# The transposes of the attention probabilities move behind the projections of queries and keys within a slot

## What is computed

```python
def attention(q, k, v, mask):
    scores = jnp.einsum('bhqd,bhkd->bhqk', q, k) / jnp.sqrt(jnp.float32(HD))
    scores = scores * mask - 10000.0 * (1.0 - mask)
    probs = jax.nn.softmax(scores, axis=-1)
    return jnp.einsum('bhqk,bhkd->bhqd', probs, v)
ln_out = layernorm(hidden_states, ln1_s, ln1_b)
q, k, v = jnp.split(ln_out @ w_qkv + b_qkv, 3, axis=-1)
x = hidden_states + merge_heads(attention(..q, k, v.., ltor_mask)) @ w_ao + b_ao
ln_out = layernorm(x, ln2_s, ln2_b)
q = ln_out @ w_q + b_q
k, v = jnp.split(encoder_states @ w_kv + b_kv, 2, axis=-1)
x = x + merge_heads(attention(..q, k, v.., cross_mask)) @ w_co + b_co
ln_out = layernorm(x, ln3_s, ln3_b)
return x + gelu(ln_out @ w1 + b1) @ w2 + b2
```

## The kernel before

| engine | order |
|---|---|
| TensorE | scores, **transposes**, flips of slots 5 and 6, weighing, flip of the context (2, 3), queries (0, 2, 4) or keys (1, 3, 7), flip of slot 4, outputs, values, keys of slot 5, queries of slot 6 |
| ScalarE | top of the values, output row, **high half of the probabilities**, high halves of flips, bias and exponentials, high half of queries or keys, middle of the values, flip of slot 4, high halves of keys of slot 5 and queries of slot 6 |
| VectorE | maxima, mask, norm (4), **low half of the probabilities**, statistics (1, 2), low halves of flips, context, low half of queries or keys, flip of slot 4, low halves of keys of slot 5 and queries of slot 6, centre (1, 3), norm (3) |

## Time and profile before

### The profile page before, as it was taken

One profiled execution on the slowest core, in us unless ns is written; L12 is line 12 of the kernel. 1 busy time (PEld: TensorE's weight loads), 2 busy tenths in 40 slices (PEclk: granted clock), 3 DMA queues, 4 the chain that ended last, 5 costly groups with the idle time before them and its releaser, 6 DMA issues. The chain is left out here.

```text
span 2081.6 us, 39412 instructions
## 1 busy us (share of the span) xinstructions
PE 1957.9 (94%) x12304; PEld 1657.1 (80%) x12304; DVE 1390.2 (67%) x2571; ACT 1072.6 (52%) x2562; POOL 884.1 (42%) x910
## 2 busy tenths in 40 slices
PE   5999999999998999999999999699999999999999
PEld 5788888888787778887887887588888888888887
DVE  6889889888888998899889888662322323232221
ACT  4666666667667666666676666443222222222222
POOL 5556556556557655555565555450201012020110
PEclk9999999999999999999999999899999999999999
DMA  6332222222223432332232224501010101101010
GB/s 172 94 91 70 65 77 68 66 72 74 61 73 88 106 97 73 86 93 72 77 96 71 73 83 104 165 28 51 11 55 5 60 12 48 50 10 54 6 41 21
DMA packets 144820, 141.51 MB, mean 68 GB/s; under 512 B 20736, under 2 KB 94464, under 8 KB 144768
## 3 DMA queue, kind: packets, MB, share of 16 engines
q1 hardware_dynamic: 144768, 140.85, 24.2%
HBM read 82.07 MB, written 25.17 MB: 52 GB/s over the span
## 5 line engine op out<-in xcount | busy, mean ns | idle before, releaser
L1046 POOL TENSOR_TENSOR a_t_s<-a_t_s,a_m_add 128x512 f32<-128x512 f32 x256 | 345.4, 1349 | 334.3 <-DVE a_t_s L837 334.1
L1315 DVE TENSOR_TENSOR m_g_r<-m_g_t,m_g_r 128x512 fp32r<-128x512 f32 x128 | 95.9, 750 | 476.1 <-ACT m_g_r L1294 476.0
L1223 PE MATMUL m_ps_h<-k_bd,wt 128*128 128x512 f32 x1536 | 378.7, 397 | 2.9 <-PEq L360 2.9
L1223 PEld LDWEIGHTS m_ps_h<-k_bd,wt 128*128 128x128 f32 x1536 | 289.2, 189 | 72.4 <-issue 3.3
L1237 PE MATMUL m_ps_y<-m_down_hi,m_g_r 128*128 128x512 f32 x1024 | 343.8, 396 | 0.1
L704 ACT ACTIVATE a_p_s<-a_t_s,a_nb 128x128 f32<-128x128 f32 x1024 | 328.3, 391 | 8.3
L524 PE MATMUL a_ps_c<-a_xT,wt 128*128 128x256 f32 x2304 | 318.2, 288 | 11.6 <-DVE a_xT L885 5.5
L524 PEld LDWEIGHTS a_ps_c<-a_xT,wt 128*128 128x128 f32 x2304 | 285.4, 191 | 25.3 <-issue 10.9
L1237 PEld LDWEIGHTS m_ps_y<-m_down_hi,m_g_r 128*128 128x128 f32 x1024 | 192.4, 188 | 45.1 <-issue 0.5
L1278 ACT ACTIVATE m_g_t<-m_ps_h,bias_cols 128x512 f32<-128x512 f32 x128 | 88.1, 688 | 270.9 <-PE m_ps_h L1223 270.7
L688 ACT CAST a_pT<-a_ps_t 128x512 f16<-128x512 f32 x256 | 150.0, 586 | 150.7 <-PE a_ps_t L502 150.4
(11 more groups left out here) (85 smaller groups left out, 3210.9 us busy)
## 6 DMA issues: line engine op xcount, KB each, us to landing
k_bd<-a_k_r SPq DMA_DIRECT2D x512, 64.0 KB, 2.1
a_x_t<-in_x SPq DMA_DIRECT2D x32, 256.0 KB, 2.8
a_res_t<-in_x SPq DMA_DIRECT2D x32, 256.0 KB, 2.8
x_after_self<-a_y_t SPq DMA_DIRECT2D x32, 256.0 KB, 2.0
a_x_t<-x_after_self SPq DMA_DIRECT2D x32, 256.0 KB, 2.7
a_enc_t<-in_ctx SPq DMA_DIRECT2D x32, 256.0 KB, 2.9
raw_wt<-in_w SPq DMA_DIRECT2D x32, 256.0 KB, 4.7
a_res_t<-x_after_self SPq DMA_DIRECT2D x32, 256.0 KB, 3.9
```

The lines of the kernel that those rows point to most:

```text
L1046: nc.gpsimd.tensor_tensor(t_s[:, n % 2], t_s[:, n % 2], m_add[:, b].unsqueeze(1).to_broadcast([P, HQ, P]), ALU.add).then_inc(s["biased"], 1)
L1223: last = nc.tensor.matmul(ps_h[j % 2][:], w1[hw][:, j // KC, kc, (j % KC) * P:(j % KC + 1) * P], xT[:, hx, kc], start=(k == 0), stop=(k == ...
```

## The change

In each engine's slot function one step moves behind the columns of slots 0 to 4 and 7: TensorE's transposes of the probabilities, ScalarE's copy of their high half and VectorE's low half. On TensorE they come now behind the flips of slots 5 and 6, the weighing, the context's flip and the columns, and ahead of slot 4's flip, the outputs, the values, and the columns of slots 5 and 6. On ScalarE they come behind the exponentials and the columns' high half, and ahead of the middle of the values; on VectorE behind the statistics, flips, context and the columns' low half, and ahead of slot 4's flip, the centring and the columns of slots 5 and 6. Nothing else differs: the same instructions with the same waits.

```diff
@@ TensorE @@
                         if cur:
                             scores(g, n)
-                        if cur if n >= 2 else prev:
-                            transpose_probs(*lag(g, n, 2))
                         if n == 5 and nxt:
                             (flip_enc if crosses(g + 1) else flip_x)(g + 1, 1)
...
                         if n == 7 and nxt:
                             keys(g + 1, 1)
+                        if cur if n >= 2 else prev:
+                            transpose_probs(*lag(g, n, 2))
                         if n == 4 and nxt:
@@ ScalarE @@
                             output_row(g - 1, (n - 5) // 2)
-                        if cur if n >= 2 else prev:
-                            high_probs(*lag(g, n, 2))
                         if n in (2, 3) and prev:
...
                             high_cols(g + 1, 1, WK, k_r, "k_done", "kh_done")
+                        if cur if n >= 2 else prev:
+                            high_probs(*lag(g, n, 2))
                         if n in (1, 3) and cur:
                             value_middle(g, n // 2)
@@ VectorE @@
                             norm(g + 1, 1)
-                        if cur if n >= 2 else prev:
-                            low_probs(*lag(g, n, 2))
                         if n in (1, 2) and ahead:
...
                             low_cols(g + 1, 1, WK, k_r, "kh_done", "kl_done")
+                        if cur if n >= 2 else prev:
+                            low_probs(*lag(g, n, 2))
                         if n == 4 and nxt:
```

## The result

The kernel after takes 2107.53 us (median of 4 runs, 2106.79 to 2108.84) against 2081.70 for the kernel before in the same comparison: ratio 1.0123, 95% interval [1.0108, 1.0137]. It is slower by 1.2%. Its profiled execution spans 2106.9, 25.3 more than before.

The account below looks back on a forecast made before the run. A ring of TensorE (leg 1), ScalarE and VectorE (leg 2) and VectorE (leg 3) was taken to set each group's period. 15 SELF at +0.90 and 15 CROSS at +0.42 made 19.8 us, so 2100.5, range 2071 to 2113.

Parts of the forecast that it names:

- Leg 3, slot 3: VectorE, slot 1's centring to slot 5's flip: in slot 3 it idles behind the late weighing, +1.23 us a group.
- Slot 3's wait on TensorE: Sign of being right: TensorE idle about 1 us before slot 3's weighing, where the wait was small.
- Leg 3, slot 4: VectorE's context multiplication starts inside GpSimd's mask addition and ends earlier: -0.64 us a group.
- Leg 1: TensorE from slot 5's flip to the next group's slot 1 weighing: SELF +0.25 us, CROSS -0.23 us.
- slot-7 wait: TensorE's keys in slot 7 wait for VectorE's low half without transposes to cover it: +0.25 us.
- CROSS queries: TensorE's queries in CROSS slot 6 no longer wait for a flip's low half: -0.48 us.
- four as before: 0: Four sets of transposes stay between slot 5's flip and slot 1's weighing on TensorE, so no change.
- Leg 2: ScalarE and VectorE, from slot 1's weighing to slot 1's centring: 0, bounds -0.3 and +0.3 us.
- the first and last ones partial: 15 and 15: Of 16 groups of each kind, 15 SELF at +0.90 and 15 CROSS at +0.42 were counted: 19.8 us.
- VectorE comes first: Rival: a centring in slot 1 or 3 starts before GpSimd's last third, 0.9 us less a group, 2073.5; chance 0.17.
- The slack takes it: Rival: free order within VectorE's slots absorbs the waits, no change, 2079 to 2085, say 2081; chance 0.14.
- The gain of slot 4 doesn't come: Rival: slot 4's multiplication still falls behind GpSimd's second addition, +0.59 in place of -0.64, 2137; chance 0.07.

Follow-up runs that it names:

- Run 11: Kernel after with slot 3 in its old order on TensorE, ScalarE and VectorE: 2088.93 us, ratio 1.0021.
- run 1: Kernel before with only VectorE's low half of the probabilities moved behind the columns, in slot 4 alone: 2065.4 us, ratio 0.9909.
- run 2: Kernel after with slot 2 in its old order on TensorE, ScalarE and VectorE: 2084.14 us, ratio 1.0005.
- run 7: Kernel before with the change made in slot 2 alone on TensorE, ScalarE and VectorE: 2100.65 us, ratio 1.0081.
- run 9: Kernel before with only the first of GpSimd's two residual additions moved, from slot 4 to slot 5: 2054.3 us, ratio 0.9860.
- run 6: Kernel before with both GpSimd residual additions moved from slots 4 and 6 to slots 5 and 7: 2076.25 us, ratio 0.9963.
- run 8: Kernel after with both GpSimd residual additions moved from slots 4 and 6 to slots 5 and 7: 2161.32 us, ratio 1.0369.
- run 5: Kernel after with VectorE's statistics (slots 1 and 2) moved behind the context and its moments behind the low half: 2104.78 us, ratio 1.0104.
- run 10: Kernel after with only the first GpSimd residual addition moved from slot 4 to slot 5: 2113.44 us, ratio 1.0143.
- run 3: Kernel after with slot 7 in its old order on TensorE, ScalarE and VectorE: 2103.74 us, ratio 1.0092.
- run 4: Kernel after with the old order in the slots where weights are split, on TensorE, ScalarE and VectorE: 2103.68 us, ratio 1.0099.

## Why the prediction came near, point by point

**Leg 3, slot 3**: right, term by term. Forecast +1.23: 0.75, 0.40 and 0.08. These are delays of a start. Measured are 0.65 idle ahead of the flip and 0.30 ahead of the keys, and an instruction that follows an idle time also loses the 0.08 to 0.09 by which VectorE's instructions overlap otherwise, so the delays are 0.73 and 0.38; the last one is 0.06 (the low half, at 414.07, overlaps the keys' by 0.02 in place of 0.08). That is 1.17. With the centring (+0.05 for +0.06) and slot 4 (-0.63 for -0.64) these add up to +0.59; the leg as a whole, forecast at +0.65, came out at +0.63 (16.16 less 15.53). Run 11 shows the cause: with something else beside the chain the 0.65 goes.

That this leg sets the period is seen across the runs. Read in the same way in group 9, it differs from the kernel before by -0.64 in run 1, -0.17 in run 2, +0.60 in run 7, -1.05 in run 9 and -0.06 in run 11, and the period by -0.54, -0.05, +0.61, -0.94 and +0.05. Runs 6 and 8 fall out, since their rows come late in slot 1 and leg 2 is longer: -1.05 and +0.63 for -0.24 and +2.00.

**Slot 3's wait on TensorE**: forecast about 1, measured 0.37, since the weighing in slot 2 had already waited 0.42. Run 5, in which slot 2's is gone, has about 0.89 in slot 3. The prediction did not name the wait in slot 2. It cost nothing in the steady groups.

**Leg 3, slot 4**: right, the mechanism shown by runs 1, 9 and 10; forecast -0.64 a group, and 0.54 to 0.66 less alone.

**Leg 1**: the slot-7 wait was forecast at +0.25 and is +0.25 (run 3 takes it back). The CROSS queries were forecast at -0.48, and slot 6 is 0.63 shorter. The leg from the flip (421.87) to the weighing in slot 1 is 17.94, where it was 17.86 (from 410.36): +0.08 and not +0.25. What was mis-sized is "four as before: 0", at the two ends of the leg. Slot 1's transposes left it, which is worth 0.44: the weighing comes 0.70 behind the scores of slot 1, 1.14 before. Slot 5's came in, and there the time from the flip to the scores of slot 6 grew by 0.26 only (421.87 to 425.90, 4.03; 410.36 to 414.13, 3.77). In the slots between nothing was gained or lost but the wait of slot 7. Why slot 5 takes the transposes so cheaply was not followed up. The scores of slot 6 and the weighing in slot 1, of the kernel after and of the kernel before:

```profile
425.90 0.86 PE L492 MATMUL a_ps_s<-k_bd,a_q_r 128*128 128x512 f32 x3
...
439.81 0.53 PE L515 MATMUL a_ps_o<-a_v_b,a_pT 128*128 128x97 bf16 x8
```

```profile
414.13 0.86 PE L492 MATMUL a_ps_s<-k_bd,a_q_r 128*128 128x512 f32 x3
...
428.22 0.52 PE L515 MATMUL a_ps_o<-a_v_b,a_pT 128*128 128x97 bf16 x8
```

In group 9 that is most of what the steady period is short of the forecast. Over the steady groups the period is longer by 0.58 to 0.72 for +0.90 in SELF and by 0.10 to 0.22 for +0.42 in CROSS.

**Leg 2**: 0, as forecast, and by the mechanism named (the centring ends 0.55 behind GpSimd's last third). The forecast had it start 0.04 behind GpSimd's start; it starts 0.66 behind and still ends there. But the prediction didn't see that the low half had been covering a DMA: "SP only gets the keys' placement later ... so 0" looked at the scores that read the keys, not at the loads queued behind the placement, nor at VectorE's statistics, which come earlier now. In a steady group that wait of 0.67 was hidden by GpSimd. In groups 2 and 18 it was not.

**The sum**: the total came near by luck, and this is the step that failed: "the first and last ones partial: 15 and 15" priced the groups at the beginnings like all others. The prices were too high in the steady groups (24 of them: 12 by 0.90 and 12 by 0.42 is 15.8, measured 10.1) and far too low in groups 0 to 2 and 15 to 18 (at the forecast's prices 4 by 0.90 and 3 by 0.42, 4.9; measured 16.1; this counts one SELF group more than the forecast's 15). There the weights of the next stage are split and loaded, and the step was moved past that work on all three engines; runs 4 and 5 give part of it back, in groups 1, 15 and 17 and in groups 2 and 18. Two errors of 5.7 and 11.2 us in opposite directions, with the smaller terms, left the sum 5.5 below the span of 2106.9 (2101.4 was forecast for it). The mechanism of the steady groups was forecast; that their too high prices would make up for half of what the beginnings cost was not.

**Rivals.** *VectorE comes first* fell, and its price was wrong as well. In the kernel after 32 centrings start 0.04 behind GpSimd's last third and take 1.62 to 1.64; one starts 0.15 ahead of it and takes 0.74. In run 7 the centring does come first, 0.15 ahead, and takes 0.74; but then the norm behind it is held by the same addition and takes 1.61. From the centring's start to the norm's end it is 2.27 (406.74 to 409.01), and 2.24 with GpSimd first, in the kernel before (402.60 to 404.84):

```profile
404.10 0.74 DVE L924 SCALAR_TENSOR_TENSOR a_xn<-a_xn,a_rstd,norm_row 128x512 f32<-128x512 f32 x1
```

Winning that race was worth nothing, since a second instruction of the same kind stands behind. *The slack takes it*: in part. Steady slots 2 and 3 show that TensorE's waits replace each other (run 5), but VectorE's idle time is real. *The gain of slot 4 doesn't come*: fell, by the 0.72.

The Trainium skill, "SBUF — State Buffer", section "Who interferes with whom", has a VectorE instruction with two SBUF inputs contend with a GpSimd instruction that reads SBUF, and calls the port pair that they share an exclusive lock. The traces agree: the multiplication takes 1.35 when it starts 0.07 behind the residual addition, 0.29 in run 9, where GpSimd is idle beside it, and 0.71 in run 10, where it starts inside the mask addition and no addition follows.

## What to carry to other kernels

When several engines wait for each other in a ring, find the engine that has no slack in it and ask of a moved step only what it does to that engine's order; a wait that shows on another engine can move by a slot at no cost (run 5). Look at what the moved step was covering, a DMA among it, on each engine that it is moved past, and price the groups at the beginnings by themselves, since other work stands in the same slots there. Don't take the time from one start to the next for the price of a step: here it fell from 0.44 to 0.35, and the step behind took the difference. And test a move slot by slot: here it was worth +17 us in slot 2 by itself, -8 in slot 6 of one kind of group (on top of run 9), and VectorE's part of it alone -18 in slot 4.

## What was not expected of the hardware

- Which of VectorE and GpSimd holds the other turns on less than 0.15 us, and the one that starts first by the profile is not always the one that holds. Against GpSimd's last third (128x512), centrings that started 0.01 to 0.02 ahead of it were still held (1.68 to 1.70, one case in each of four kernels, among them), and those 0.15 ahead were not (0.74). Where between the two it turns isn't shown. Beside a smaller GpSimd addition (128x1, line 1025) 0.05 to 0.06 ahead was enough: 0.73 or 0.74, 29 cases in run 6, and there GpSimd's addition took 1.09 in place of 0.55.
- An instruction that starts inside one GpSimd addition gets in ahead of the next one, though that one follows at once: 0.72 and 0.71 for a multiplication of 0.29 (0.71 too where none follows, run 10), and the residual addition behind it then takes 1.33 to 1.35 in place of 1.26.
- Four transposes take 0.35 from start to start behind the columns and 0.44 behind the scores, with the same operands, and the slot is no shorter (slots 0, 1 and 6: +0.03, 0, -0.01).
